# A graph network kernel: node blocks of 128 in columns, one program for three stages, chunks of 512 nodes

## The reference, cut to what matters

```
for each edge, both ways:   m = W3 relu(W2 relu(W1 [x_from, x_to, feature] + b1) + b2) + b3
agg  = sum of m over the edges into each node (both ways)
s1 = gru0(x, agg);  s2 = gru1(agg, s1);  s3 = gru2(s1, s2)        # three cells, 128 wide
x1 = layernorm(x + s3)
X  = x1
for l in 0..2:   Z = (1+eps_l) X + A X;   X = relu(Z W1_l + b1_l) W2_l + b2_l    # A: edge counts, 3125 x 3125
out = layernorm(x1 + X)
```

## Time and profile before

| | us |
|---|---|
| median of 3 runs (2384.44 to 2385.42) | 2384.72 |
| profiled execution, its own time | 2386.11 |
| its span, first to last instruction | 2384.4 |
| PE busy (95%) | 2270.8 |
| PE weight loads (79%) | 1879.7 |
| DVE busy (75%) | 1786.1 |
| ACT busy (52%) | 1231.1 |
| POOL busy (49%) | 1157.7 |

### The profile page before, as it was taken

One profiled execution on the slowest core, in us unless ns is written; L12 is line 12 of the kernel. 1 busy time (PEld: TensorE's weight loads), 2 busy tenths in 40 slices (PEclk: granted clock), 3 DMA queues, 4 the chain that ended last, 5 costly groups with the idle time before them and its releaser, 6 DMA issues. The chain is left out here.

```text
span 2384.4 us, 39642 instructions
## 1 busy us (share of the span) xinstructions
PE 2270.8 (95%) x12547; PEld 1879.7 (79%) x12547; DVE 1786.1 (75%) x4056; ACT 1231.1 (52%) x2106; POOL 1157.7 (49%) x846
## 2 busy tenths in 40 slices
PE   4999999999999999999999999999999879799996
PEld 3888888888888888888888888888887645588885
DVE  7888888888888888888888888888887556602114
ACT  4556656656656666566665666666655314211112
POOL 2566656666666566665666666666665400000000
PEclk9999999999999999999999999999999879799999
DMA  4355545445445444554454554544544550395873
GB/s 158 72 122 114 108 88 102 98 88 112 97 88 111 88 103 97 96 111 89 95 105 88 111 98 89 110 89 99 102 95 93 64 219 1 125 390 229 335 288 144
DMA packets 233138, 292.58 MB, mean 123 GB/s; under 512 B 126815, under 2 KB 190661, under 8 KB 224599
## 3 DMA queue, kind: packets, MB, share of 16 engines
q1 hardware_dynamic: 159556, 237.05, 32.5%
q0 software_dynamic: 73216, 54.58, 17.3%
q10 hardware_dynamic: 272, 0.05, 0.0%
HBM read 218.51 MB, written 73.08 MB: 122 GB/s over the span
## 5 line engine op out<-in xcount | busy, mean ns | idle before, releaser
L473 POOL DMA_INDIRECT sums<-outb,target x416 | 665.7, 1600 | 603.8 <-ACT outb L644 438.5
L466 POOL DMA_INDIRECT xg<-in_x,gidx x416 | 487.3, 1172 | 148.5 <-issue 135.2
L1241 PEld LDWEIGHTS ebank<-w3t,h 128*128 128x128 f32 x3328 | 387.4, 192 | 8.3 <-issue 0.3
L1241 PE MATMUL ebank<-w3t,h 128*128 128x128 f32 x3328 | 388.2, 275 | 0.2 <-ACT h L626 0.2
L1229 PE MATMUL ebank<-h1h,w2h 128*128 128x512 f32 x832 | 365.4, 439 | 3.3 <-DVE h1l L853 3.3
L626 ACT ACTIVATE h<-ebank,b2c 128x512 f32<-128x512 f32 x416 | 286.6, 689 | 124.0 <-PE ebank L1229 98.8
L612 ACT ACTIVATE h1h<-hpre 128x512 fp32r<-128x512 f32 x416 | 258.0, 628 | 177.9 <-DVE hpre L849 135.2
L1229 PE MATMUL ebank<-h1h,w2l 128*128 128x512 f32 x832 | 328.6, 395 | 0.0
L1229 PE MATMUL ebank<-h1l,w2h 128*128 128x512 f32 x832 | 326.4, 392 | 0.0
L853 DVE SCALAR_TENSOR_TENSOR h1l<-hpre,h1h 128x512 fp32r<-128x512 f32 x416 | 268.7, 687 | 17.3 <-ACT h1h L612 14.7
L849 DVE TENSOR_TENSOR hpre<-pb,ebank 128x512 f32<-128x512 f32 x416 | 265.0, 676 | 3.2 <-PE ebank L1215 2.0
(11 more groups left out here) (266 smaller groups left out, 3778.5 us busy)
## 6 DMA issues: line engine op xcount, KB each, us to landing
ring<-adj SPq DMA_DIRECT2D x54, 1568.0 KB, 8.0
rowb<-along SPq DMA_DIRECT2D x104, 512.0 KB
ef<-in_edge_attr SPq DMA_DIRECT2D x103, 256.0 KB
adj<-band SPq DMA_DIRECT2D x48, 480.0 KB
adj<-band SPq DMA_DIRECT2D x24, 540.0 KB
stay<-adj SPq DMA_DIRECT2D x6, 1568.0 KB, 14.3
xg<-in_x,gidx POOLq DMA_INDIRECT x416
sums<-outb,target POOLq DMA_INDIRECT x416
```

Of the source, the lines that this page charges most:

```text
L466: pool.indirect_dma_start(out=to, out_offset=None, in_=a["x"], in_offset=bass.IndirectOffsetOnAxis(ap=ids, axis=0)).then_inc(s_x[par], 16)
L473: pool.indirect_dma_start(out=tables[k % 2], out_offset=bass.IndirectOffsetOnAxis(ap=target[par][:, 1, k:k + 1], axis=0), in_=outb[par][:, ...
L1241: last = nc.tensor.matmul(bank[6 + way][:, t * P:(t + 1) * P], h2[:, way, k, t * P:(t + 1) * P], w3t[:, k, :], start=not bias and k == 0, ...
```

## The change

1. **Numbering.** A block is 128 nodes in a row: block b holds nodes 128b to 128b+127, the last one 53. Blocks in a transposed tile are 128 neighbouring columns (`block_cols`), panel b of `adj` is 128 neighbouring rows of DRAM. Node rows of x, of the tables and of the output go between DRAM and SBUF in pieces of 512 bytes (`by_block`).
2. **Chunks.** 6 chunks of 512 nodes and one of 64 (`chunk`, `width`) in place of 7 of 448, for b3, cells, layers and norms.
3. **One program.** One block holds all three stages, with shared banks (`Seam`) and tiles at fixed places (`Slab`); waits on single semaphores stand where the barriers were.
4. **End of the edge stage.** SP, not ACT, sends and fetches the degrees; then SP waits for the table additions, loads the tables group by group (14 DMAs), and only then flushes the last three pieces of the band (one more than before). SP's loop of rounds is written out. PE transposes the out-degrees. ACT no longer clears x1 at the start.
5. **Start of the cells.** ACT copies weights and x out of the banks, POOL adds the tables group by group, PE transposes a group of sums inside the chunks of the first cell, and a cell does its x matmuls ahead of its h matmuls.
6. **Norms.** PE starts each group when its chunk is done; root and scaling run in two halves; one or two groups are scaled on ACT.
7. **Layers.** (1+eps) x1 of layer 0 is 25 matmuls of x1 with the diagonal, straight into the banks. The ring is filled during the cells. DVE empties a bank when its last panel product is done (`s_lane`), W2 matmuls wait for their own chunk. x1 + b2 less its mean goes to POOL (the mean's sum stays on DVE, in layer 1).

```diff
-NP = 125
-NB = N // NP
+NB = -(-N // P)
+TAIL = N - (NB - 1) * P
-CH = 448
+CB = 4 * P
+HALVES = ((0, 16, (0, 1, 2, 3)), (16, NB, (4, 5, 6)))
...
+            def sums_in():
+                for j, (b, nb) in enumerate(GROUPS):
+                    for k, tab in enumerate(tabs):
+                        sp.dma_start(tab[0:rows_in(j), b:b + nb, :], by_block(tables[k], b, nb)).then_inc(seam.s_tab[j], 16)
...
-                with sp.Fori(0, ROUNDS) as m:
...
+                for g in range(10, G - 1):
...
+                sp.wait_ge(s_deg, 2)
+                sp.dma_start(degrees[0, 0:QS * PACE].rearrange("(q r) -> q r", r=PACE), indegs[0:QS, :]).then_inc(s_degst, 16)
+                sp.dma_start(degrees[1, 0:NB * P].rearrange("(b p) -> b p", p=P), outdegs[:, :]).then_inc(s_degst, 16)
...
+                for t in range(2):
+                    sp.wait_ge(s_add[t], G * 2 * 16)
+                sums_in()
+                for b in range(ITERS - 3, ITERS):
                     sp.wait_ge(s_acc, G * 2)
...
+def block_cols(t, b):
+    return t[:, b * P:min((b + 1) * P, N)]
+def by_block(x, b, nb):
+    if b + nb < NB:
+        return x[b * P:(b + nb) * P, :].rearrange("(b p) d -> p b d", p=P)
+    return x[b * P:N, :].unsqueeze(1)
+def panels_of(adj_flat):
+    return adj_flat[0:NR * AW, :].rearrange("(b p c) o -> p b (c o)", p=P, c=AW)
...
+    @block.gpsimd                                       # gru_stage
+    def _(pool):
+        for j, (b, nb) in enumerate(GROUPS):
+            pool.wait_ge(seam.s_tab[j], 2 * 16)
+            r = rows_in(j)
+            nc.gpsimd.tensor_tensor(tab0[0:r, b:b + nb, :], tab0[0:r, b:b + nb, :], tab1[0:r, b:b + nb, :],
+                                    ALU.add).then_inc(s_sumtab, 1)
...
+        def cell(c, n, seq):                            # PE
+            for j in range(3):
+                nc.tensor.matmul(bank[4 * par + j][:, 0:w], wt[:, c, 0, j, :], chunk(x, n), start=True, stop=(j == 2))
+            if seq == 0:
+                sums_out(0)
+            if c == 0 and n + 1 < NGR:
+                sums_out(n + 1)
+            if c:
+                pe.wait_ge(s_cell, (c - 1) * NGR + n + 1)
+            else:
+                pe.wait_ge(s_total, n + 1)
+            for j in range(2):
+                last = nc.tensor.matmul(bank[4 * par + j][:, 0:w], wt[:, c, 1, j, :], chunk(h, n), start=False, stop=True)
...
+        pe.wait_ge(s_wz, 2)                             # sum_stage, PE
+        for j, (b, nb) in enumerate(GROUPS):
...
+            for t in range(nb):
+                cut = P if j < NGR - 1 else width(j)
+                nc.tensor.matmul(lane(j)[:, t * P:t * P + cut], x1[0:r, b + t, :], wz[0:r, 0, 0:cut],
+                                 start=(t == 0), stop=False)
...
+                            if end and n < NGR - 1:
+                                last.then_inc(s_lane, 1)
```

More of the change, by code:

```diff
@@ L170, in edge_stage @@
         shift = sb("shift", [P, 3, K])
-        bank = [ctx.enter_context(nc.psum_tensor(f"ebank{i}", [P, 512], fp32)) for i in range(8)]
+        band = sb("band", [P, NB * BAND])
+        target = [sb(f"target{i}", [P, 3, K], i32) for i in range(2)]
+        outb = [sb(f"outb{i}", [P, K, D]) for i in range(2)]
+        sdh = sb("sdh", [P, 3, GE], f32r)
+        hpre = sb("hpre", [P, HB, 2, GE])
+        b3r = sb("b3r", [P, D])
+        indegs = sb("indegs", [P, PACE])
+        fits = sb("fits", [1, 1], i32)
+        outdegs = sb("outdegs", [NB, P])
+        lower = sb("lower", [P, P])
+        column = sb("column", [P, P])
+        spots = sb("spots", [P, GE], f16)
+        place = sb("place", [P, 1])
+        count_i = sb("count_i", [P, GE + 4], i32)
+        keys = sb("keys", [P, G, 2, K])
+        away = sb("away", [P, G, K])
+        rowkey = sb("rowkey", [P, G, K])
+        colkey = sb("colkey", [P, G, K])
+        blkkey = sb("blkkey", [P, G, K])
+        colhot = sb("colhot", [P, K, WIDER], bf16)
+        h1h, h1l, h2 = hidden
         rows_i = pb[0:G, :, :].bitcast(i32)
@@ L1325, in into_each @@
                     pe.wait_ge(s_hot, G)
+                    pe.wait_ge(s_deg, 1)
+                    transpose(bank[2][0:NB, P:2 * P], outdeg[:, 2, :], P)
                     for j in range(BEFORE + 1):
@@ L1413, in _ @@
                 general()
[L1418 to L1451, removed]
@@ L1454, in norm_scalar, with width @@
[L1454 to L1463, removed]
[L1464 to L1471 removed]
+def width(j):
+    return min(CB, AW - j * CB)
@@ new lines, in chunk, with rows_in, __init__, begin @@
+def chunk(t, j):
+    return t[:, j * CB:j * CB + width(j)]
+def rows_in(j):
+    return P if j < NGR - 1 else TAIL
+def block_cols(t, b):
[6 more added lines that the diff above has]
+    return adj_flat[0:NR * AW, :].rearrange("(b p c) o -> p b (c o)", p=P, c=AW)
+class Slab:
+    def __init__(self, nc, ctx, name, size):
+        self.nc, self.size = nc, size
+        self.base = -(-nc.sbuf_base // 32) * 32
+        ctx.enter_context(nc.sbuf_tensor(name, [P, size // 4], fp32))
+    def begin(self):
+        self.at = 0
+    def take(self, name, shape, dt=fp32):
+        t = self.nc.alloc_sbuf_tensor_at(name, [P] + list(shape), dt, offset=self.base + self.at)
+        self.at += -(-int(np.prod(shape)) * 4 // 32) * 32
+        assert self.at <= self.size
+        return t
```

1084 lines of the change are left out of this document (593 added, 491 removed).

## The result

The changed kernel takes **2328.07 us** (median of 4 runs, 2326.39 to 2330.84); the kernel before took 2384.58 beside it (4 runs, 2380.03 to 2385.42). The ratio is 0.9768, interval 0.9751 to 0.9785: 2.3% faster. The forecast was 2328; that the median meets it to 0.1 us is partly luck, for the four runs lie 4.5 us apart. The profiled execution has a span of 2324.6 and a time of its own of 2326.39, so about 1.8 us lie outside the span.

The account below looks back on a forecast made before the run. PE bounds the edge loop, so the gain must come from the 493 us behind it. Seven pieces, 1892.5 + 23.8 + 96.4 + 27.7 + 225.5 + 34.0 + 27.5, sum to 2327.4; forecast 2328 us, range 2313 to 2343.

Parts of the forecast that it names:

- B: From PE's last sum to the end of the first cell: 23.8 us where it was 56.9; bounds 18 to 36 for the gain.
- E: Three product phases: 75.2 us each, +3 in all, loads and PE nearly level; bounds -2 to +8.
- A: Edge loop up to PE's last sum at 1891.5: +1 us for loading x in 512-byte pieces; between 0 and 6.
- the two branches: Start of the cells: PE's transposes with ACT's copies ready at 1908.4, beside POOL's additions and SP's first table group at 1906.
- the rule that 512 bytes suffice for line rate: Table loads before the first cell: by the skill's rule about 1.3 us a group, not 3, ending the piece 2 us sooner.
- C: Cells 2 to 21: 96.4 us where they took 90.2, the short chunk a pure loss; bounds 94 to 100.
- D: From the last cell through the norm to the first product: 27.7 us where it was 40.9; bounds 23 to 33.
- this wait, which the prediction named: Norm: PE waits until 18.9 us for the diagonal, made only behind the norm; 50 passes of 7.7 us follow.
- the rival of slow panel loads: Products: neighbouring-row panels load worse, kernel slower than before; at 250 GB/s 2424 us. Chance 0.05 together with a late SP list.
- F: Two passages between layers: 17.0 us each where each was 24.2, -14.4 in all; bounds 33 to 40 for both.
- The rival that the stride has nothing to do with it: Norm and W2 matmuls: weights stay at 0.24 us a pass, 11.9 for 50; +20 us, kernel 2348. Chance 0.06.
- G: The end, behind the last products: 27.5 us where it was 34.1, output starting at 18.3; bounds 25 to 31.

Follow-up runs that it names:

- The equal chunks: Changed kernel with only the cells back to 7 equal parts of 448 columns; 2324.93 us, ratio 0.9732 to the kernel before.
- The early diagonal: Changed kernel, but DVE makes the diagonal of 1+eps before the first root of the norm; 2323.87 us, ratio 0.9735 to the kernel before.
- the run with both relieved: Changed kernel without the products' 64-column passes except in the last panel, and loading only two of three ring tiles anew; 2309.88 us.
- the run on strides: Changed kernel with W2 weights taken at every 2nd, 8th and 24th column by layer, and neighbouring columns in the norm; 2344.38 us.

## Why the prediction was right, step by step

The waits that the change was to take off the path are gone in every piece. Two steps of the mechanism were not as predicted: the clock of the b3 matmuls (B), and who sets the pace of the products (E). Single terms were off by up to 4 us and made up for each other, in B above all; that part of the match is luck.

**A.** The prediction allowed 1 us for the load of x in short pieces; 0.8 came, which is less than the edge loop's own spread and so confirms no more than that the loop isn't slower. PE's last sum ended between 1890.5 and 1897.0 in the traces of the changed kernel's variants, and that spread, in a part that none of these edits touches, is as large as the whole spread of a kernel's single runs.

**B.** 23.6 against 23.8, but by errors that cancel. The joint between the stages was kept at 4.3 us; it is 0, so leaving the branch cost PE nothing that shows, and the 4.3 went with the barrier. The b3 matmuls were put at 5.4 and took 8.1 (1892.21 to 1900.35): the granted clock is 0.87 over 1892 to 1896 and 0.50 over 1896 to 1900, so it fell at about 1895, within them, though PE had been busy without a gap. The prediction expected it to fall in an idle joint. This is no accident of one execution. In all ten traces in which these matmuls follow PE's last sum without a gap, the clock is 1.00 at the first of them and 0.50 at the last, and they take 6.3 to 8.6 us; in the run without the 64-column passes it fell latest, in the window from 1900 on (0.69), and they took 6.3. What sets them apart is that weights and moving operand have two rows (2*128, 2x512); at 1906 to 1908, behind transposes of 128 rows, the clock is 1.00 again. That the rows are the cause was not tested.

POOL's last addition was forecast for 1898.3 and came at 1900.81, since an addition takes 3.4 us to land (the DMA view's median at 1900 to 1906) and the next to the same table waits for it; SP issued the tables at 1904.25, not at 1902. Against that the tables moved faster than the 175 GB/s that I took: 298. The last to arrive at the first h matmul is POOL's second addition: PE waits 1.51 us for it, and without it DVE's first addition (1911.18 + 0.69) would have been last, 1.3 us sooner than the 1913.15 at which the h matmuls start. In the prediction the two branches lay 1 us apart, with PE's last. The rate was mis-sized, and it didn't decide the sum: with 1.8 us a group POOL's adds of 1.26 follow at some 1.65 from the second on, far inside a cell's 5.2. One slip of the working lies in B as well: 1897.9 for the end of b3 is 5.4 behind 1892.5, which holds the 1 us of A, while the 23.8 is counted from 1891.5, so that 1 us stands in the sum twice.

On the rule that 512 bytes suffice for line rate (the Trainium skill, DMA: Bandwidth & Descriptors, Specifications), the measurement stands in between: 298 GB/s at a DMA share of 1.03, twice the 480-byte writes and three quarters of the 396 to 420 that long pieces reach here.

**C.** 97.0 against 96.4. The two gaps behind short chunks, put at 1 us each, are 0.9 each; one of 0.9 at a transpose of sums in the first layer was not forecast, and is the 0.6 and a bit that the piece is over. The equal chunks return 3.3 of the 6.8 that it lost against before; of the other 3.5 the transposes of sums, which moved into the cells, are 2.4 by the prediction's count.

**D.** 25.8 against 27.7. DVE's last scaling comes 17.3 us behind the last cell, not 18.4, the opening matmuls take 8.0, not 7.7, and the branch costs 0, not 1. The order in it is as forecast: scaling, diagonal, matmuls. The early diagonal shows that this wait, which the prediction named, was 4 to 5 us.

**E.** The sum was right (226.5 against 225.5), its ground only partly. I had the loads and PE level, with the loads setting most of the phase; PE sets it. A panel takes 75.05 / 25 = 3.00, not 2.97: by the run with both relieved a 512-column pass costs (69.01 - 2 x 0.126) / 300 = 0.229 where I took 0.2275, and a 64-column fp32r pass 0.126 where I took the 0.12 of an fp32 one. The loads add 0.1 to 0.8 a phase. At 396 GB/s they run as before, so the rival of slow panel loads falls.

**F.** 16.8 each against 17.0. W2's 50 passes take 5.77, as forecast from neighbouring columns; the earlier trace rows had 11.94. The rival that the stride has nothing to do with it falls with the run on strides. A price of a weight load by its number of columns alone (the Trainium skill, TensorE: Matmul & The Clock Gate, LDWEIGHTS) misses a factor of 2.2 here: 0.25 against 0.115 for the same 128 columns. What makes it isn't shown.

**G.** 25.8 against 27.5. W2 ended at 11.3, as forecast; the output started at 17.0 and not 18.3, since DVE's passes took 11.6 us (2305.28 to 2316.84) and not 13.5.

Of the gain of 59.8 us in span, B gave 33.3, D 15.1, F 14.8 and G 8.3, while A, C and E cost 11.7. Open are what in the b3 matmuls lets the clock fall, how much of B's gain is the barrier's alone, and what in the chip makes the step between strides of 8 and 32 bytes.

## What to carry to other kernels

When a program's stages are joined, look at what the barrier waited for. Here the order of one queue and the barrier hid each other: the order alone lost 2 us, all the rest of the change with the old order gained 4 in piece B, both together gained 33. Keep the fp32 weights of a matmul in neighbouring columns, or at most every second one (0.115 and 0.126 us a pass here, against 0.24 and more). Before cutting work at the hardware's largest size, price the remainder: 6 x 512 + 64 costs as many weight loads as 7 x 448, and it costs an extra wait wherever a neighbour's work was the cover.

## What the hardware showed that was not expected

- The price of a strided read of weights is no straight line: 0.115 us for a pass with neighbouring columns, 0.126 at stride 8 bytes, 0.242 at 32 and 0.25 at 96.
- A store of 12 KB has landed 1.4 us after its issue where the DMA share is 0.2 to 0.4; behind three stores of 480-byte pieces its issue alone occupied SP's queue for 10.06 us, after these had occupied it for 17.14.
- 512-byte pieces read from DRAM at 298 GB/s, 480-byte pieces are written at 146 to 149, both at a DMA share above 1.
- The clock fell to half within b3's matmuls of two rows, in all ten traces where they follow other work without a gap, although PE was busy 4.00 of 4 us before and while it fell.
